# Masked attention on one Trainium2 core: turning the probabilities ahead of the next scores in steps 0 and 2

## The reference, cut to what matters

```
def attention(q, k, v, mask):
    scores = jnp.einsum('bhqd,bhkd->bhqk', q, k) / jnp.sqrt(jnp.float32(HD))
    scores = scores * mask - 10000.0 * (1.0 - mask)
    probs = jax.nn.softmax(scores, axis=-1)
    return jnp.einsum('bhqk,bhkd->bhqd', probs, v)

ln_out = layernorm(hidden_states, ln1_s, ln1_b)
qkv = ln_out @ w_qkv + b_qkv
q, k, v = jnp.split(qkv, 3, axis=-1)
ctx = merge_heads(attention(split_heads(q), split_heads(k), split_heads(v), ltor_mask))
attn_out = ctx @ w_ao + b_ao
x = hidden_states + attn_out
ln_out = layernorm(x, ln2_s, ln2_b)
q = ln_out @ w_q + b_q
kv = encoder_states @ w_kv + b_kv
k, v = jnp.split(kv, 2, axis=-1)
ctx = merge_heads(attention(split_heads(q), split_heads(k), split_heads(v), cross_mask))
cross_out = ctx @ w_co + b_co
x = x + cross_out
```

## Time and profile before

| | |
|---|---|
| median of 3 runs | 2399.71 us |
| the profiled execution | 2399.77 us, its span 2398.1 us |
| TensorE busy in the span | 2195.2 us (92%) |
| VectorE | 1787.8 us (75%) |
| ScalarE | 1447.0 us (60%) |
| GpSimd | 710.9 us (30%) |
| masked stage | from about 1545 to 1925 us of the span |

### The profile page before, as it was taken

How to read it: one execution, slowest core, us unless ns; L and a number is a source line. 1 busy time by engine, 2 the same in 40 slices (tenths; PEclk the granted TensorE clock), 3 DMA queues, 4 the chain that set the end, 5 groups by cost and what they waited for, 6 DMA issues and landing times. The chain is left out here.

```text
span 2398.1 us, 52415 instructions
## 1 busy us (share of the span) xinstructions
PE 2195.2 (92%) x17289; PEld 1772.5 (74%) x17289; DVE 1787.8 (75%) x4688; ACT 1447.0 (60%) x4012; POOL 710.9 (30%) x995
## 2 busy tenths in 40 slices
PE   5999999998999999996989999789998969799998
PEld 4898989997899989996975665456666569466664
DVE  6666666667666666666758999698888766699986
ACT  3554545554555555554737778577777756288875
POOL 2111111112211111102024655466666610243400
PEclk8999999999999999998979999799999989599999
DMA  5000011100100001002000000100000000000001
GB/s 128 23 23 24 23 24 46 35 17 7 23 23 23 23 23 23 1 1 70 0 7 10 11 9 6 36 8 1 6 18 16 10 5 0 10 13 8 9 4 36
DMA packets 72953, 47.25 MB, mean 20 GB/s; under 512 B 29232, under 2 KB 71601, under 8 KB 72753
## 3 DMA queue, kind: packets, MB, share of 16 engines
q1 hardware_dynamic: 72752, 44.62, 7.0%
HBM read 41.45 MB, written 2.10 MB: 18 GB/s over the span
## 5 line engine op out<-in xcount | busy, mean ns | idle before, releaser
L1912 DVE TENSOR_REDUCE maxima<-bank 128x2 f32<-128x512 f32 x512 | 332.5, 681 | 34.9 <-PE bank L1005 33.2
L1547 ACT ACTIVATE probs_t<-bank 128x512 f32<-128x512 f32 x512 | 282.4, 600 | 66.8 <-PE bank L996 65.3
L1421 ACT ACTIVATE wide_probs_t<-bank 128x256 f32<-128x256 f32 x256 | 98.4, 384 | 299.6 <-PE bank L881 297.4
L1426 ACT ACTIVATE wide_probs<-bank,wide_neg_max 128x129 f32<-128x129 f32 x512 | 184.1, 365 | 116.9 <-DVE wide_neg_max L1759 113.2
L2264 POOL TENSOR_TENSOR wide_columns<-wide_pair_columns,zero 128x8 f32<-128x8 f32 x16 | 3.3, 206 | 740.2 <-DVE x L1791 697.5
L1433 ACT ACTIVATE wide_heads_high<-bank,wide_columns 128x128 fp32r<-128x128 f32 x512 | 160.2, 365 | 88.1 <-PE bank L895 86.5
L1764 DVE RECIPROCAL wide_inverse<-wide_sums 128x2 f32<-128x2 f32 x256 | 42.4, 166 | 226.2 <-ACT wide_probs L1426 226.2
L1766 DVE TENSOR_SCALAR wide_probs<-wide_probs,wide_inverse 128x128 f32<-128x128 f32 x512 | 177.5, 389 | 9.0
L1778 DVE SCALAR_TENSOR_TENSOR wide_heads_low<-bank,wide_columns,wide_heads_high 128x128 fp32r<-128x128 f32 x512 | 154.9, 344 | 36.2 <-ACT wide_heads_high L1433 31.3
L1005 PE MATMUL bank<-k_packed,q_packed 32*128 32x256 f32 x1024 | 175.9, 344 | 3.7 <-ACT q_packed L1532 2.2
L1583 ACT ACTIVATE probs<-scores_masked,neg_max 128x128 f32<-128x128 f32 x512 | 163.3, 394 | 24.8 <-DVE neg_max L2095 23.2
(11 more groups left out here) (302 smaller groups left out, 6840.7 us busy)
## 6 DMA issues: line engine op xcount, KB each, us to landing
cn<-in_ctx SPq DMA_DIRECT2D x48, 128.0 KB, 2.0
wide_pair_weights<-in_L_xattn_wq SPq DMA_DIRECT2D x16, 256.0 KB, 2.8
wide_pair_weights<-in_L_xattn_wk SPq DMA_DIRECT2D x16, 256.0 KB, 3.2
wide_pair_weights<-in_L_xattn_wv SPq DMA_DIRECT2D x16, 256.0 KB, 3.6
wide_pair_weights<-in_L_xattn_wo SPq DMA_DIRECT2D x16, 256.0 KB, 3.4
q_packed<-max_rows SPq DMA_DIRECT2D x256, 4.0 KB
wide_ctx_rows<-in_ctx SPq DMA_DIRECT2D x4, 512.0 KB, 6.7
x<-in_x SPq DMA_DIRECT2D x4, 512.0 KB, 7.7
```

The costliest lines, as they stand in the source:

```text
L1426: last = act.activation(probs0[:, b, h, :], wide_scores[b % 2][:, h * KEYS0:(h + 1) * KEYS0], ACT.Exp, bias=neg_max0[:, b, h:h + 1], accum ...
L1547: act.activation(probs_t[j % 8][:, :], shifted_bank[j % 2][:, :], ACT.Exp, bias=0.0).then_inc(s.exp_ready, 1)
L1912: dve.tensor_reduce(maxima[pack // 2][:, b, pack % 2, :], head_scores[packed_scores(1 - u, j)][:, :].rearrange("p (a k) -> p a k", a=UNITS ...
```

## The change

In TensorE's program of the masked stage, in each step, the block of the turns (L1189) is put ahead of the block of the scores (L1182). It makes a difference in steps 0 and 2 alone, which have both. The conditions and the waits of each block stay as they are. In window 0 the steps 0 and 2 have no turn.

```
 for j in range(STEPS):
     g = STEPS * n + j
-    if core and j % 2 == 0:
-
-        pe.wait_ge(s.spread, 2 * n + j // 2 + 1)
-        after(pe, s.masked, g)
-        for r in range(2):
-            half = slice(r * P // 2, (r + 1) * P // 2)
-            pe.matmul(score_bank[r][:, :], qk[u][half, j // 2, :], km[u][half, j // 2, :], start=True, stop=True)\
-              .then_inc(s.scores, 1)
     if core and j == 3 or past and j < 3:
         pe.wait_ge(s.exp_ready, g - 2)
         after(pe, s.probs_copied, g - 3)
         t = (j - 3) % STEPS
         for m in range(PACK):
             last = pe.transpose(turn_bank[:, m * P:(m + 1) * P], probs[t][:, m * P:(m + 1) * P], ident[:, :])
         last.then_inc(s.probs_turned, 1)
+    if core and j % 2 == 0:
+        pe.wait_ge(s.spread, 2 * n + j // 2 + 1)
+        after(pe, s.masked, g)
+        for r in range(2):
+            half = slice(r * P // 2, (r + 1) * P // 2)
+            pe.matmul(score_bank[r][:, :], qk[u][half, j // 2, :], km[u][half, j // 2, :], start=True, stop=True)\
+              .then_inc(s.scores, 1)
```

More of the change, by code:

```diff
@@ L1175, in window @@
                     g = STEPS * n + j
+                    if core and j == 3 or past and j < 3:
+                        pe.wait_ge(s.exp_ready, g - 2)
+                        after(pe, s.probs_copied, g - 3)
+                        t = (j - 3) % STEPS
+                        for m in range(PACK):
+                            last = pe.transpose(turn_bank[:, m * P:(m + 1) * P], probs[t][:, m * P:(m + 1) * P], ident[:, :])
+                        last.then_inc(s.probs_turned, 1)
                     if core and j % 2 == 0:
@@ L1183, in window @@
                               .then_inc(s.scores, 1)
[L1184 to L1190, removed]
                     if late and j == 1:
```

## The result

The changed kernel takes 2409.22 us (median of 5 runs, 2408.86 to 2415.04) where the kernel before takes 2398.91 (5 runs, 2393.16 to 2400.63): a ratio of 1.0054, 95% interval 1.0039 to 1.0069. It is slower by 0.4 to 0.7%. Timed a second time, it came out at 2413.21 against 2400.00, ratio 1.0059 (1.0037 to 1.0081).

A forecast was written before the change was run, and what follows sets the result against it. TensorE was taken as nearly full (166.4 of 186, 172.0 of 189 us), its few waits circling with VectorE. Delays of 9.6, 1.0, 0.2, 1.9 and 0.9 made 13.6 us, so 2399.8 became 2413.4; range 2402 to 2424.

The forecast's parts named there:

- the projection's small waits: TensorE's values projection waits for VectorE's later addition to x: up to 0.1 us in a dozen windows, 0.9 together.
- The turn's data is there: Steps 0 and 2: the turn starts where the scores started, its exponential and emptied bank ready, without a new wait.
- rival 3: Step 2: the turn waits 0.76 us for an exponential in each of 31 windows, giving 2437.0; chance 0.05.
- The shift: Steps 0 and 2 on TensorE: scores come 0.49 us later, turned probabilities 1.07 earlier; changed load neighbours taken as nothing.
- Odd step 0: Odd windows: later scores delay the mask pass and vn, so the turn of the heads comes 0.47 us later.
- odd step 2: Odd windows: the mask pass moves 0.49 us, and the next even window's turn of the heads moves by all of it.
- no second count of even step 2: Even windows, step 2: the mask pass moves 0.49 us, the same 0.49 that reaches the odd window's vn; counted once.
- Even step 0 is covered: Even windows, step 0: the 0.49 us shift of the scores is hidden by VectorE's older work, costing nothing.
- In the cross half it is the even window's step 2 that is paid through VectorE: Cross windows, step 0: VectorE too full to be idle carries 0.49 us from the even window's step 2, paying as much.
- Rivals 1 and 2: Before the second turn: copy wait gone, 8.9 us faster, chance 0.10; odd gains cancel even losses, 2399 to 2402, chance 0.12.
- Rival 4: Even windows: longer TensorE waits bring more clock falls, 4.8 us on top for three, 22 for all fourteen; chance 0.07.

The follow-up runs named there:

- step 2 alone: The kernel before with the turns put ahead of the scores in step 2 only, step 0 keeping scores first: 2407.70 us, ratio 1.0034.
- `vn` first: VectorE's pass for vn put ahead of the mask pass of step 0: in the kernel before 2385.02 us, in the changed kernel 2396.43 us.
- the repetition: The changed kernel as it stands, timed and profiled again beside the kernel before: 2413.21 us, ratio 1.0059.

## Why the prediction was right

- *The stage* was forecast 13.6 us longer and is 13.9 as measured; the time 2413.4 and measured 2409.2, then 2413.2. That the two stage figures lie 0.3 apart is luck. The swap itself costs 12.3, so the sum was 1.3 too high, and the fall in window 32 and the start of the stage, which the sum didn't have, added 1.6.
- *The terms*: windows 0 to 7 were given 0.2 + 1.0 and cost 1.3; the ten pairs from window 8 to 27 were given 9.6 and cost 9.0 (0.90 each, not 0.96); windows 28 on were given 1.9 and cost 2.0 without the fall. The 0.9 for the projection's small waits should not have been a term of its own: they are part of the 0.90.
- *The turn's data is there*: held. From 1560 to 1919 no turn waits at all, and rival 3 is out.
- *The shift* of 0.49 was mis-sized: 0.43 in odd step 0. The loads were taken as alike; a turn's takes 0.14 us and a score's 0.18, and with the neighbours changed the scores come 0.06 sooner than reckoned. The price of a place was nearly right (0.46 measured, 0.47 and 0.49 said) since the projection behind the addition to x waits as well, 7.5 us of load waits in 28 places. In window 14 it starts 2.37 us after the projection of step 2 and not 2.26 (1716.69 to 1719.06; 1712.52 to 1714.78), and at the next scores 0.05 of this is left: they start 8.64 us behind the turn of the heads of window 14 and not 8.16, which is 0.43 + 0.05. Less the 0.02 of slack it is 0.46.
- *Odd step 0*, *odd step 2* and *no second count of even step 2* in the self half: held. 11.11 became 11.57 and 12.09 became 12.55. That both steps count, and that they add to within 0.9 us, is shown by the runs of one step each (4.4 and 8.8).
- *Even step 0 is covered*: shown by the swap there alone, +0.4 us over 16 windows, and this from window 30.
- *In the cross half it is the even window's step 2 that is paid through VectorE*: borne out by step 2 alone (0.49 a self pair, 0.87 a cross pair) and by the 0.84 a pair that remain there with `vn` first. I used this in the sum and forgot it in the expectation for the changed kernel with `vn` first.
- *Rivals 1 and 2* (faster, no difference) needed slack in `vn`. It had 0.02 us, and the waits went there. With that slack made (`vn` first) an early turn does pay, where the scores are covered too.
- *Rival 4* (more falls of the clock): the falls in windows 20 to 26 did not become more, one before (window 20) and one after (window 26). The waits of 1.47 and 1.70 us that the change made in late even windows brought no more of them. The fall in window 32 is one more than before and costs 1.05 us; it is in both profiles of the change. The prediction looked for more falls in even windows only, not in the drain of the pipeline, and that this one is of the change's making is not shown.

What failed to come out by the numbers given: the forecast took the whole to move with the stage. In the first pair of profiles over 4 us less came through, and the stages behind it had a higher granted clock there; in the profile of the repetition they had not, and 13.1 came through. Whole times at mean clocks from 0.956 to 0.966, spread by up to 12 us, don't tell kernels apart that differ by 4.

## What to carry to other kernels

When an engine runs in order and is almost full, moving ready work ahead changes who is late, not how much is done: name the consumer of what is moved back and look up its slack before crediting the gain of what is moved forward. A wait of 0.5 us that a reordering removes is worth nothing if the next wait on the same engine has 0.02 us of slack. And the order pays once the later consumer is served first: here a 0.4 us pass moved ahead on VectorE was worth 10.6 us, and 5.4 more then came from the very reordering that had cost 12.3, restricted to the places where the delayed work was covered and with one more turn moved up. And look for falls of the clock before comparing two traces, at the stretch's ends too: here they and the start of the stage made 1.6 of the 13.9 us.

## What the runs showed of the hardware that I had not expected

- A group of transposes behind a projection starts 0.89 us after it (1720.02 to 1720.91, after), a group of score matmuls 0.99 (1715.74 to 1716.73, before). The first load of the transposes shows 0.11 ahead of their matmul; the scores' load shows within 0.01 of theirs, in both orders.
- Executions of one program vary with the clock: the change again took 2415.3 and 2415.9 us at a mean granted clock of 0.956 and 0.957, and 2409.2 and 2409.8 at 0.962. The stage's length in two profiles of it agreed to 0.02 us; both have the same two falls and the same start.
- The clock ahead of a stage shows inside it: with a granted clock of 0.68 to 0.70 in the 2 us ahead of the first scores (three profiles) the second scores followed 3.2 us later, with 1.00 (eight profiles) 3.75.
